# Depthwise convolution and rotation over 16 images: channels in another order on the partitions, second-half granules loaded by quarters, one store a step on SyncE's queue

## The reference

```python
x = x + conv5x5_depthwise(_gn(x), kernel(L0_conv_weight))         # padding 2, one 5x5 kernel per channel
x = x + einsum('hvc,bchw->bvhw', rota_matrix[:64], _gn(x))        # for each image row h a 128x128 matrix over channels
```

## Time and profile before

| | us |
|---|---|
| median of 3 runs | 466.86 (466.16 to 467.9) |
| the profiled execution, its own time | 464.26 |
| its span in the profile | 462.5 |
| PE busy | 411.2 (89%) |
| DVE busy | 361.8 (78%) |
| ACT busy | 264.6 (57%) |
| POOL busy | 241.8 (52%) |
| moved by DMA | 139.82 MB, mean 302 GB/s |

### The profile page before, as it was taken

How to read it: one execution, slowest core, us unless ns; L and a number is a source line. 1 busy time by engine, 2 the same in 40 slices (tenths; PEclk the granted TensorE clock), 3 DMA queues, 4 the chain that set the end, 5 groups by cost and what they waited for, 6 DMA issues and landing times.

```text
span 462.5 us, 8597 instructions
## 1 busy us (share of the span) xinstructions
PE 411.2 (89%) x3110; PEld 202.4 (44%) x3110; DVE 361.8 (78%) x691; ACT 264.6 (57%) x513; POOL 241.8 (52%) x312
## 2 busy tenths in 40 slices
PE   8899999999999999999999999999976056999930
PEld 2355555555555555444444444454432022444410
DVE  4899999999999998999998988987656022887830
ACT  2467767667567568667677665667342005777700
POOL 7597667567567567666666654562111204445400
PEclk9999999999999999999999999999998566999985
DMA  8736777999986889798999899999999997999998
GB/s 306 310 78 205 264 232 227 324 344 371 290 293 202 230 284 383 293 345 279 365 299 372 298 328 387 316 348 333 387 351 146 223 206 99 347 412 427 425 428 337
DMA packets 36698, 139.82 MB, mean 302 GB/s; under 512 B 7552, under 2 KB 7680, under 8 KB 24448
## 3 DMA queue, kind: packets, MB, share of 16 engines
q1 hardware_dynamic: 16272, 107.28, 66.9%
q10 hardware_dynamic: 20384, 31.99, 22.6%
HBM read 72.14 MB, written 67.12 MB: 301 GB/s over the span
## 4 chain that ended last, share of the span: by engine, by line
PE 81%; DMA 10%; POOL 2%; SPq 1%; issue 1%; DVE 1%; ACT 1%; ACTq 0%; POOLq 0%
PE ps L740 57%; PE ps L775 22%; DMA x_scratch<-area 8%; POOL area L444 2%; DMA kept<-x_scratch 2%; PE ps L781 1%; ACT gn L539 0%; PE ps L750 0%; SPq L284 0%; PE ps L758 0%; SPq L259 0%; POOL area L458 0%; DVE tin L649 0%; DVE area L597 0%; DVE gn L586 0%
## 5 line engine op out<-in xcount | busy, mean ns | idle before, releaser
L740 PE MATMUL ps<-area 64*64 64x496 f32 (+2 forms) x2560 | 281.4, 586 | 1.9 <-POOL area L444 1.9
L740 PEld LDWEIGHTS ps<-area 64*64 64x64 f32 x2560 | 140.5, 133 | 97.6 <-issue 87.7
L444 POOL TENSOR_TENSOR area<-mask,area 128x325 f32<-128x325 f32 x128 | 132.5, 1058 | 44.2 <-PE ps L740 32.9
L775 PE MATMUL ps<-gn,rot 128*128 128x512 f32 x256 | 121.1, 627 | 25.8 <-issue 13.9
L518 ACT ACTIVATE area<-area,affine 128x256 f32<-128x256 f32 x192 | 97.9, 588 | 31.9 <-DVE affine L629 29.9
L531 ACT ACTIVATE area<-ps 64x512 f32<-64x512 f32 x128 | 75.8, 592 | 30.2 <-PE ps L740 24.2
L775 PEld LDWEIGHTS ps<-gn,rot 128*128 128x128 f32 x256 | 49.6, 200 | 94.5 <-issue 76.4
L607 DVE BATCH_NORM_STATS2 stats<-area 128x6 f32<-128x512 f32 x128 | 80.6, 689 | 3.9 <-DMA area<-in_x_dram 3.9
L616 DVE BATCH_NORM_STATS2 stats<-area 128x6 f32<-128x512 f32 x128 | 81.0, 696 | 1.1
L458 POOL TENSOR_SCALAR area<-area,affine 128x256 f32<-128x256 f32 x62 | 46.1, 754 | 57.1 <-DVE affine L629 57.0
L649 DVE TENSOR_TENSOR tin<-ps,tin 128x512 f32<-128x512 f32 x72 | 49.0, 690 | 33.0 <-PE ps L775 33.0
(11 more groups left out here) (26 smaller groups left out, 109.4 us busy)
## 6 DMA issues: line engine op xcount, KB each, us to landing
area<-in_x_dram SPq DMA_DIRECT2D x31, 1024.0 KB, 7.8
x_scratch<-area ACTq DMA_DIRECT2D x58, 512.0 KB, 8.7
tin<-x_scratch SPq DMA_DIRECT2D x18, 1024.0 KB, 12.3
out_dram<-tin SPq DMA_DIRECT2D x17, 1024.0 KB, 11.5
out_dram<-area SPq DMA_DIRECT2D x10, 1024.0 KB, 24.4
rot<-in_rota_dram SPq DMA_DIRECT2D x4, 1024.0 KB, 10.6
area<-x_scratch SPq DMA_DIRECT2D x4, 1024.0 KB, 27.7
out_dram<-kept SPq DMA_DIRECT2D x4, 1024.0 KB, 20.9
```

The source lines that it names most:

```text
L444: last = nc.gpsimd.tensor_tensor(taps[k % TRING][:, c * KW:(c + 1) * KW].rearrange("p d (b r) -> p d b r", r=TAPS), mask[:].rearrange("p d ...
L740: last = nc.tensor.matmul(ps[half, bank + c].rearrange("p (j w) -> p j w", j=J)[:, :, outs], taps[k % TRING][rows, (2 * pair + c) * KW + d ...
L775: nc.tensor.matmul(ps[:, rot_bank(m), :], rot[:, n % UNITS * RH + h], gn[n % NRING][:, h], start=True, stop=True).then_inc(rotated, 1)
```

## The change

Four things change; the arithmetic and the order of work on PE, DVE and POOL stay.

1. Channels on the partitions of a granule stand in another order. Partition p = 4i + r holds the channel that is the (32r + i)th in the scratch, so a quarter r of the scratch's channels (four groups of the convolution) lies on every fourth partition. In the scratch, too, the channels of a group alternate between its two halves of partitions. The rotation matrix is permuted to match by the host's layout, and the output is put back.
2. The store of x1 is one transfer of 128 partitions a group, issued by SP in every step, instead of two of 64 by ACT.
3. Granules 16 to 22 are loaded by quarters of 32 channels: for 16 to 19 quarter 0 in steps 22 to 25, quarter 1 in steps 26 to 29, quarter 2 in steps 30 and 31; for 20 to 22 quarters 0 to 2 after the loop; quarter 3 of all seven behind the last x1 store. 23 and later are loaded whole after that.
4. Granules 13 to 15 are loaded at steps 29 to 31 into x buffers that are free by then; other granules change buffers accordingly.

```diff
         def store(queue, k):
             queue.wait_ge(x1_ready, 2 * (k + 1))
-            half = k // PER_HALF
-            for n in range(2):
-                first = k % PER_HALF * 2 * GC + n * GC
-                rows, dst = slice(n * HALF, (n + 1) * HALF), x1_dram[half, first:first + GC]
-                if k > 0:
-                    queue.dma_start(dst.rearrange("c h j w -> h c (j w)"), x_of(k)[rows].rearrange("p c j w -> p c (j w)")
+            g = k % PER_HALF
+            dst = x1_dram[k // PER_HALF, g * 2 * GC:(g + 1) * 2 * GC].rearrange("(c n) h j w -> (n h) c (j w)", n=2)
+            if k > 0:
+                queue.dma_start(dst, x_of(k).rearrange("p c j w -> p c (j w)")).then_inc(x1_stored[k % XRING], 16)
...
+        def load_granule(queue, n):
+            rows = slice(n % UNITS * RH, (n % UNITS + 1) * RH)
+            queue.dma_start(tin[n].rearrange("c h x -> c (h x)"),
+                            x1_dram[n // UNITS, :, rows].rearrange("(r i) h j w -> i r (h j w)", r=QUARTERS)
+                            ).then_inc(in_landed[n], 16)
+
+        def load_quarter(queue, n, r):
+            rows, channels = slice(n % UNITS * RH, (n % UNITS + 1) * RH), slice(r * QUARTER, (r + 1) * QUARTER)
+            queue.dma_start(tin[n][r:C:QUARTERS].rearrange("c h x -> c (h x)"),
+                            x1_dram[n // UNITS, channels, rows].rearrange("c h j w -> c (h j w)")
                             ).then_inc(in_landed[n], 16)
...
-                sp.wait_ge(x1_ready, 2 * (s - 1))
+                store(sp, s - 2)
...
+                n = s - 29 + KEPT
+                if KEPT <= n < UNITS:
                     await_stores(sp, s - 3)
                     sp.wait_ge(stats_ready, measured(s - 3 + LAG))
-                    load_granule(sp, EARLY[s - EARLY_STEP], slice(0, EARLY_CHANNELS))
...
+                load_granule(sp, n)
+
+                for r, steps in ((0, (22, 23, 24, 25)), (1, (26, 27, 28, 29)), (2, (30, 30, 31, 31))):
+                    for n in range(FRONT):
+                        if steps[n] == s:
+                            await_stores(sp, PER_HALF + (r + 1) * PER_QUARTER - 1)
+                            load_quarter(sp, UNITS + n, r)
...
-                store(act, s - 1)
...
-    rota = _np.ascontiguousarray(_np.asarray(inputs['L1_conv_rota_matrix'], dtype=_np.float32).transpose(2, 0, 1))
+    order = _channels()
+    rota = _np.asarray(inputs['L1_conv_rota_matrix'], dtype=_np.float32).transpose(2, 0, 1)
+    rota = _np.ascontiguousarray(rota[order][:, :, order])
```

More of the change, by code:

```diff
@@ L303, in load_norms @@
             def load_norms(half):
-                channels = NORM2_BATCH[half] * 2 * GC
                 sp.wait_ge(norm2_stored, 32 * (half + 1))
-                sp.dma_start(norm2[0:channels, half], norm2_dram[half, 0:channels]).then_inc(norm2_landed, 16)
+                for r in range(QUARTERS):
+                    count = min(max(NORM2_BATCH[half] * 2 * GC - r * QUARTER, 0), QUARTER)
+                    if count:
+                        sp.dma_start(norm2[r:QUARTERS * (count - 1) + r + 1:QUARTERS, half], norm2_dram[half, r * QUARTER:r * QUARTER + count]
+                                     ).then_inc(norm2_landed, 16)
             def load_x(k):
@@ L364, in _ @@
-            sp.wait_ge(convolved, 2 * STEPS_ALL)
[L365 to L372, removed]
+                    load_granule(sp, n)
+                for r, steps in ((0, (22, 23, 24, 25)), (1, (26, 27, 28, 29)), (2, (30, 30, 31, 31))):
[3 more added lines that the diff above has]
+                            load_quarter(sp, UNITS + n, r)
@@ new lines, in _ @@
+            sp.wait_ge(out_stored[9], 16)
+            for r in range(QUARTERS - 1):
+                load_quarter(sp, 20, r)
+            await_stores(sp, STEPS_ALL - 3)
+            sp.wait_ge(stats_ready, measured(STEPS_ALL - 3 + LAG))
+            for r in range(QUARTERS - 1):
+                load_quarter(sp, 21, r)
+            store(sp, STEPS_ALL - 1)
+            store_granule(sp, 11)
+            sp.wait_ge(out_stored[10], 16)
+            for r in range(QUARTERS - 1):
+                load_quarter(sp, 22, r)
@@ L552, in _ @@
             evict(1, 0)
-            store(act, 0)
             for s in range(FILL, STEPS_ALL - 1):
@@ L830, with _channels @@
 _OUTS = [((B, C, H, W), 'float32')]
+def _channels():
+    order = []
+    for p in range(C):
+        place = p % QUARTERS * QUARTER + p // QUARTERS
+        step, c, n = place // (2 * GC), place % (2 * GC) // 2, place % 2
+        order.append(step * 2 * GC + n * GC + c)
+    return order
 def _laid_out(inputs):
@@ L874 @@
     got = _np.asarray(r.results[0]["out_0_dram"]).reshape(2, UNITS, C, RH, J, W)
-    return _np.ascontiguousarray(got.transpose(0, 4, 2, 1, 3, 5)).reshape(B, C, H, W)
+    got = got.transpose(0, 4, 2, 1, 3, 5).reshape(B, C, H, W)
+    back = [0] * C
+    for p, c in enumerate(_channels()):
+        back[c] = p
+    return _np.ascontiguousarray(got[:, back])
```

95 lines of the change are left out of this document (36 added, 59 removed).

## The result

| | before | changed |
|---|---|---|
| median, us | 466.51 (466.1 to 467.9, 4 runs) | 446.0 (441.78 to 448.2, 4 runs) |
| ratio, 95% interval | | 0.9545 (0.9466 to 0.9623) |
| profiled execution, us | 464.26 | 441.78 |
| its span | 462.5 | 439.9 |
| forecast | | 432, range 426 to 446 |

What follows compares the result with a forecast made beforehand. PE bounds the convolution, slow transfers the middle, bytes the end. The last store goes at 344.2 us, then 34.1 MB at 422 GB/s take 80.8, to 425.0; 2.4 quiet give span 427.4, plus 1.76 and 2.6 about 432, range 426 to 446.

Steps and rivals of the forecast that it cites:

- the full queue: Rival, convolution stage: SyncE's one queue overfills, x or granules come late, PE has gaps; 439 to 444 us, chance 0.15.
- The convolution stage at nothing: Convolution stage: transfers of each step fit within PE's step, so moving the stores to SyncE's queue costs nothing.
- The margin of the second half: Second half of the convolution: steps 22 to 29 ask 11.7 us of the queue in a 12.5 us step.
- The last group: End of convolution: granule 13 comes earlier, so the last x1 store is issued at 340.6 and landed at about 346 us.
- What is late next: After the last store: PE starts granule 16 at about 354 us, DVE takes to 409, DMA to 425.0.
- The bytes: After the last x1 store: 34.1 MB remain, at 422 GB/s 80.8 us, from 344.2 to 425.0.
- Price of a store: One 128-partition x1 store of 1.05 MB takes 3.6 us, between ends of 2.5 and 5.0 us.
- Cause of the slow middle: Between convolution and last stage: 6.2 MB ahead and transfers on neighbouring partitions reaching few ports cause waits of 30.7 and 7.2 us.
- the 35 us: Whole gain: first 9.85 MB faster saves 30.5 us, two MB fewer save 4.7, together 35.2.
- Far rows: Rival, whole-granule loads: neighbouring rows 4 MB apart in the scratch load slower; 480 us at half rate, chance 0.06.
- Clock: Rival, after the last store: PE's clock stays low; at half speed PE alone ends at 464; chance no more than 0.03.
- Median against profile: Final sum: the runs' median lies 2.6 us above the profiled execution, taking 429.2 to 431.8.

Runs made afterwards that it cites:

- e1: Changed kernel with each step's x1 store issued by SyncE ahead of that step's x load instead of behind it: 431.92 us, ratio 0.9251.
- e3: Changed kernel with the one 128-partition x1 store issued by ACT at its old place, SyncE waiting only for x1_ready: 432.23 us, ratio 0.9261.
- e5: Kernel of e1 with channels in natural order, so a quarter lies on 32 neighbouring partitions: 438.02 us, ratio 0.9373.
- e6: Kernel of e1 with each x1 store split into two transfers of 64 partitions on SyncE's queue: 436.75 us, ratio 0.935.
- e7: Kernel of e1 with granules 13, 14 and 15 loaded at step 31, step 32 and right ahead of the last store: 438.18 us, ratio 0.9372.
- store-first: The kernel of e1, changed kernel with the x1 store ahead of the x load: 431.92 us; run again beside other experiments, 432.05 us.

## Why the prediction was right, and where not

**The number: inside the range by luck.** 446.0 is the range's last value, and that end had been set for the full queue, which did not come. What brought the time there is the 8.8 us before 200 us, a cost that the prediction put at nothing, the 3.7 behind the convolution and 1.6 between profile and median, together the 14 above 432.

**The convolution stage at nothing: wrong, 8.8 us.** The step that failed is "In the first half a step has 2.5 + 3.6 = 6.1 us of 8.66", and earlier in its paragraph "nothing new is waited for except their turn in one queue". I set transfer times against the step. But SyncE waits for a landing, and the wait encloses the x load queued ahead of that store: 2.5, 3.6 and some 2.4 of landing are 8.5, with 0.4 of issue 8.9. All parts but the issue stood in my text, the 2.4 at its end; I did not add them along the one path that turns. How the 8.5 divide is my estimate: measured are the whole (8.5) and 6.2 us for an x load with nothing ahead of it. e1 and e3, which open the loop in two ways, both give the loss back. Of the 8.8 us 6.9 are PE's wait and 1.8 the half clock behind it.

**Full queue: not what happened.** PE has no gap from 200 us to its last convolution, and 320 to 340 ran at 389 GB/s. The margin of the second half was real; the one that was missing lay in the first, where the queue has idle time.

**The last group: right in shape, 8 us late in time.** The store is issued 2.0 us after the last convolution matmul (forecast 2.5), and in e1 within 0.3 us of the time given. Its landing was mis-sized: 8.9 us in the changed kernel and 7.0 in e1, against 5.5.

**What is late next: right.** PE starts granule 16 at 365.4 and 355.4 (e1; forecast 354), the DMA end decides, 16.3 us behind PE's last rotation and 20.1 in e1 (forecast: from 409 to 427.4, 18.4, though the prediction's last paragraph says 17).

**The bytes: right, with a term too small.** 419 to 428 GB/s hold from 370 on, but not at once as I had taken it: after the store's issue the windows of five us have 363, 340, 308 and 352. Against 422 that is (59 + 82 + 114 + 70) x 5 / 422 = 3.9 us, against 3.7 that were missing. The likely reason, not tested by itself: SyncE stands before the store's landing from 354.6 to 357.8 and issues nothing, and then 0.26 MB quarters at 0.6 us of issue each barely feed the queue (a DMA share of 0.84 from 358 to 361).

**Price of a store: right.** It lands in 5.3 us when it is first in the queue; less a landing of about 2 that is 3.3, taken as 3.6. The 3.7 that the 3.6 came from is a slip: 44.3% of 20 us for 2.40 MB makes 3.9 for 1.05.

**Cause of the slow middle: three parts shown.** Undoing the order on the partitions (e5) costs 6.1 us, undoing the whole stores (e6) 4.8 and undoing the early granules (e7) 6.3, each alone against store-first. Store-first itself ran on two other chips (431.92 and 432.05), and the kernel before was 0.7 us slower beside e5 to e7 than beside e1, so these prices hold to about a microsecond. How the rest of the 35 us divides was not tried. One reading of the earlier trace rows is to be put right: of the five slices four move 99 to 223 GB/s, the first still 351.

**Far rows: no.** In e1 the windows from 360 to 370, with whole loads 4 MB apart in flight, run at 423 and 426 GB/s, and e5, with 128 KB between neighbours, is no faster later on. The Trainium skill's row on power-of-two pitches ("Latency and other measured facts", DMA: Bandwidth & Descriptors) gives half the rate at 4 MiB of that at 512 KiB, which the prediction had read as 480 us; here, where only groups of four neighbours lie 4 MB apart, the measurement decides against that reading.

**Clock.** It fell twice. At 190 it cost 1.8 us, as told above, in the stage where PE sets the pace; the prediction had looked for a low clock behind the last store alone. The second time it was 0.50 of full (1.2 GHz) from 365 to 371, after a wait of 3.3 us, and full again from 372. That cost nothing as far as the order of ends shows, since DMA ends 16.3 us behind PE. In e1 it is full from 170 to 200 and from 320 to 375.

**Median against profile.** I added 2.6 us. It was 4.2: the four executions spread over 6.4 us, and the profiled one was the fastest.

## What to carry to other kernels

Where an issuing engine waits for a landing and then queues work ahead of the next transfer whose landing it will wait for, add one full turn (issue, everything ahead in the queue, the transfer, the landing) and compare that with the step; the share of bytes says nothing of it. Issue first what someone waits for, and wait for it as late as you can. A gap of PE is to be priced with the low clock that may follow: here 1.8 us behind one of 6.9. A partial load should lie across the partitions, and what is left for the moment of the last dependency should be small.

## What the runs showed of the hardware

With loads on 32 neighbouring partitions 350 to 360 us ran at 205 to 218 GB/s (e5), the same ten us with every fourth partition at 372 and 349 (e1); one load on 16 neighbouring partitions ran at 73 with its latency (the kernel before). A 1 MB store of 2 KB pieces over 128 partitions landed in 5.3 us with nothing ahead of it (e1) and in 8.5 behind an x load (the changed kernel); as two halves it held the queue 2.0 us longer (e6). The issue of a quarter load took SyncE 0.6 us on every fourth partition and 0.42 on 32 neighbours (e1, e5); 0.6 us is as long as its 0.26 MB take to move. After 6.9 us of standing PE ran 3.5 us at 0.50 of its clock (the changed kernel, to 194).
